# Queries, keys and normalised x turned by transposing DMAs in a layer with differential attention

## The reference

```python
x = x + 0.5 * ffn(layernorm(x))
x = x + attn(layernorm(x))
x = x + 0.5 * ffn(layernorm(x))
```

```python
q = rope((x @ Wq).reshape(b, s, H, 2 * D)); k = rope((x @ Wk).reshape(b, s, KVH, 2 * D)); v = x @ Wv
energy = einsum('bqhad,bkhad->bahqk', q.reshape(b, s, H, 2, D), k.reshape(b, s, H, 2, D))
scores = softmax(where(causal, NEG, energy) / sqrt(D))
diff = softmax(where(causal, NEG, scores[:, 0] - lam * scores[:, 1]))
att = einsum('bhqv,bvhd->bqhd', diff, v); att = att * rsqrt(mean(att * att) + EPS) * rms_w * (1 - LAM_INIT)
return att.reshape(b, s, E) @ Wo
```

## Time and profile before

| | us |
|---|---|
| median of 3 runs | 1826.18 (1823.63 to 1830.19) |
| the profiled execution, its own time | 1838.54 |
| its span | 1836.7 |
| TensorE busy | 1473.0 (80%) |
| VectorE busy | 1456.8 (79%) |
| ScalarE busy | 1260.1 (69%) |
| GpSimd busy | 1082.6 (59%) |
| mean granted TensorE clock, share of full | 0.863 |

### The profile page before, as it was taken

One profiled execution on the slowest core, in us unless ns is written; L12 is line 12 of the kernel. 1 busy time (PEld: TensorE's weight loads), 2 busy tenths in 40 slices (PEclk: granted clock), 3 DMA queues, 4 the chain that ended last, 5 costly groups with the idle time before them and its releaser, 6 DMA issues. The chain is left out here.

```text
span 1836.7 us, 43825 instructions
## 1 busy us (share of the span) xinstructions
PE 1473.0 (80%) x10688; PEld 1035.1 (56%) x10688; DVE 1456.8 (79%) x5505; ACT 1260.1 (69%) x3426; POOL 1082.6 (59%) x1493
## 2 busy tenths in 40 slices
PE   3997645888898998889888898888988888888620
PEld 3543322666666666666666666666666666666310
DVE  5778425888889898898889988898989877674477
ACT  2363334888788888888888888888888876675320
POOL 4421443666677677776777777777777665554300
PEclk9998776788899899999999899998999887676855
DMA  8023321111111111121111111121211100001186
GB/s 304 2 64 135 118 66 42 29 32 36 32 46 46 44 50 50 44 50 44 44 44 44 44 44 50 46 52 45 51 46 45 42 19 21 19 17 41 41 312 252
DMA packets 179673, 117.30 MB, mean 64 GB/s; under 512 B 139169, under 2 KB 139553, under 8 KB 179618
## 3 DMA queue, kind: packets, MB, share of 16 engines
q1 hardware_dynamic: 179618, 116.65, 21.5%
HBM read 51.57 MB, written 33.55 MB: 46 GB/s over the span
## 5 line engine op out<-in xcount | busy, mean ns | idle before, releaser
L1675 ACT ACTIVATE ex<-bank,nbias 128x512 f32<-128x512 f32 (+3 forms) x1024 | 527.7, 538 | 83.2 <-DVE bank L1220 80.6
L1220 DVE TENSOR_SCALAR_CACHE_REDUCE bank<-bank,nesc 128x512 f32<-128x512 f32 (+3 forms) x1024 | 503.3, 551 | 84.6 <-PE bank L1930 83.9
L1960 PEld LDWEIGHTS bank<-vs,pr 128*128 128x128 f32 x2560 | 336.3, 207 | 24.5 <-issue 12.7
L1960 PE MATMUL bank<-vs,pr 128*128 (+1 forms) x2560 | 341.4, 284 | 9.8 <-DVE att L1266 5.3
L1942 PE MATMUL bank<-cst,df 128*128 128x128 f32 x1280 | 265.9, 310 | 83.6 <-ACT pr L1692 83.0
L1928 PE MATMUL bank<-ks,qs 96*128 (+2 forms) x1024 | 266.2, 337 | 68.7 <-ACT ex L1675 45.4
L1522 POOL TENSOR_SCALAR ex<-ex,gam 128x128 f32<-128x128 f32 (+3 forms) x512 | 317.3, 630 | 0.0
L1692 ACT ACTIVATE pr<-bank 128x128 f32<-128x128 f32 (+3 forms) x512 | 231.7, 453 | 88.5 <-PE bank L1942 87.3
L1246 DVE CUSTOM_DVE_ANT_0 df<-ex 128x128 f32<-128x128 f32 (+3 forms) x512 | 261.1, 525 | 8.2 <-issue 3.7
L1942 PEld LDWEIGHTS bank<-cst,df 128*128 128x128 f32 x1280 | 169.8, 167 | 111.0 <-ACT pr L1692 96.2
L1675 ACT ACTIVATION_READ_ACCUMULATOR ex<-bank,nbias 128x1 f32 x1024 | 222.6, 217 | 0.0
(11 more groups left out here) (359 smaller groups left out, 2954.5 us busy)
## 6 DMA issues: line engine op xcount, KB each, us to landing
qs<-turned SPq DMA_DIRECT2D x360, 64.0 KB, 2.1
x_dram<-xa SPq DMA_DIRECT2D x8, 1024.0 KB, 4.9
c_x<-x_dram SPq DMA_DIRECT2D x8, 1024.0 KB, 14.7
c_y<-y_dram SPq DMA_DIRECT2D x8, 1024.0 KB, 14.7
out_dram<-c_x SPq DMA_DIRECT2D x8, 1024.0 KB, 4.7
b_xs<-x_dram SPq DMA_DIRECT2D x30, 256.0 KB, 2.7
xa<-in_x SPq DMA_DIRECT2D x7, 1024.0 KB, 13.6
x<-x_dram SPq DMA_DIRECT2D x28, 256.0 KB, 2.6
```

Source lines behind the costliest of these rows:

```text
L1220: dve.tensor_scalar(part, part, nesc[:, 0:1], None, ALU.mult, ALU.min, accum_out=nbias[:, j, i, a:a + 1]).then_inc(bias_done.sem, 1)
L1675: ac.activation(ex[j % 4][:, a, lo:hi], energy(j, i)[:, a, :], ACT.Exp, bias=nbias[:, j, i, a:a + 1], scale=-1.0, accum_out=esum[:, j, i, ...
L1960: mm = pe.matmul(bank[:, 7, t * DV:(t + 1) * DV], pr[j % 2][:, lo + k * P:lo + (k + 1) * P], val, start=(k == 0), stop=(k == t))
```

## The change

The halves of x, of the queries and of the keys are turned by DMAs with the transposing flag. For queries and keys ScalarE and GpSimd write the halves in the order of the stack, four places of 32 numbers for each head and part (the fourth is filled with zeros once, ahead of everything), and one DMA turns 16 or 8 blocks of 128 x 128 straight into `qs` or `ks`. The transposes on TensorE, the copies out of PSUM, the buffer `turned` and the 24 stacking DMAs go. `stack_early` sends the first query piece in the middle of a body; the other two go at its end, and `turn_x` ahead of them. The halves of x lie in the buffer of the rotated queries (`rows`), the head norm and the second normalisation write in place, and the halves of heads and second x have a buffer of their own (`hsplit`).

```diff
-            split = sb2("split", [P, 2, NQ + NK], F16)
+            NB = (16, 16, 8)
+            split = [sb2(f"split{n}", [P, nb * P], F16) for n, nb in enumerate(NB)]
-            turned = sb2("turned", [P, 2, NC, P], F16)
+            rows = rot[:, :].bitcast(F16).rearrange("p (a n) -> p a n", a=2)
+            hsplit = sb2("hsplit", [P, 2, E], F16)
...
-            an = sb2("an", [P, E])
-            xn2, xt2 = an, at
+            xn2, xt2 = x2, at
+            def an(u):
+                return att[:, ds(u & 7, 1), :, 0:D].rearrange("p a h d -> p (a h) d")
...
+            def stacked(piece, n):
+                return piece.rearrange("p (b j d) -> p b j d", j=4, d=D)
+            def high_of(piece, n):
+                three_ = stacked(piece, n)
+                return three_[:, :, 0:3:2, :] if n < 2 else three_[:, :, 0:2, :]
+            def low_of(piece, n):
+                return stacked(piece, n)[:, :, 1 if n < 2 else 2, :]
+            def twice(ap, n):
+                return by_block(ap, n).unsqueeze(2).broadcast_to([P, NB[n], 2, D])
...
             @blk.sync
                 def load_again(u):
                     sp.wait_ge(x2_st, u * 16 + 16)
-                    xn2_done.wait(sp, u - 1, apart_s)
+                    lo2_done.wait(sp, u - 1, apart_s)
...
-                def stack(u, K, source=turned):
-                    ring, t = (u >> 2) & 1, u & 3
-                    if K is not None:
-                        e_done.wait(sp, 2 * pair(K, STEPS - 1) + 1)
-                    turned_out.wait(sp, u * 3 + 2, apart_s)
-                    for dst, order, c0, c1, done in ((qs, (0, 1, 0), 0, CQ, stacked_q),
-                                                     (ks, (0, 0, 1), CQ, NC, stacked_k)):
-                        to = dst[:, :, :].rearrange("p (r c i) (t s) -> p r c i t s", r=2, i=4, s=P)
-                        for j, part in enumerate(order):
-                            for i in range(4):
-                                sp.dma_start(to[j * D:(j + 1) * D, ds(ring, 1), :, i, ds(t, 1), :]
-                                             .rearrange("p r c t s -> p (r c) (t s)"),
-                                             source[i * D:(i + 1) * D, part, c0:c1, :]).then_inc(done, 16)
+                def turn_rows(out, source, done):
+                    for a in range(2):
+                        sp.dma_start(out[:, a, :].rearrange("p (k n) -> p k n", k=KT),
+                                     source[:, a, :].rearrange("p (k n) -> p k n", k=KT), transpose=True).then_inc(done, 16)
+                def turn_x(u):
+                    proj_done.wait(sp, 3 * u - 1, apart_s)
+                    lo_done.wait(sp, u, apart_s)
+                    turn_rows(xt, rows, xt_in)
+                def turn_part(n, ring, t, source, done):
+                    dst, first = ((qs, 0), (qs, 16), (ks, 0))[n]
+                    to = dst[:, :, :].rearrange("p (r b) (t s) -> p r b t s", r=2, s=P)[:, ds(ring, 1), first:first + NB[n],
+                                                                                       ds(t, 1), :]
+                    sp.dma_start(to.rearrange("p r b t s -> p (r b) (t s)"), source.rearrange("p (b n) -> p b n", n=P),
+                                 transpose=True).then_inc(done, 16)
+                def stack_early(u, K):
+                    e_done.wait(sp, 2 * pair(K, -1) + 1, apart_s)
+                    rlo_done.wait(sp, 3 * u, apart_s)
+                    turn_part(0, (u >> 2) & 1, u & 3, split[0][:, :], stacked_q)
+                def stack(u, K):
+                    e_done.wait(sp, 2 * pair(K, STEPS - 1) + 1, apart_s)
+                    rlo_done.wait(sp, 3 * u + 2, apart_s)
+                    turn_part(1, (u >> 2) & 1, u & 3, split[1][:, :], stacked_q)
+                    turn_part(2, (u >> 2) & 1, u & 3, split[2][:, :], stacked_k)
...
+                def turn_first(u):
+                    if u >= 2:
+                        proj_done.wait(sp, 3 * (u - 2) + 2, apart_s)
+                    lo_done.wait(sp, u, apart_s)
+                    turn_rows(p_xt[u % 2], p_rows[u % 2], first_xt[u % 2])
                 def stack_first(u):
-                    for done in (stacked_q, stacked_k):
-                        sp.wait_ge(done, u * 192 + 16)
-                    stack(u, None, p_turned[u % 2])
+                    for n in range(3):
+                        rlo_done.wait(sp, 3 * u + n, apart_s)
+                        turn_part(n, u // TB, u % TB, p_split[u % 2][n], first_stack[u % 2])
...
+                sp.wait_ge(pads_set, 6)
                 load_first(0)
                 load_first(1)
                 load_again(0)
+                turn_first(0)
+                load_first(2)
+                turn_first(1)
+                load_first(3)
...
-                load_first(2)
-                load_first(3)
+                turn_first(2)
+                load_first(4)
                 stack_first(0)
-                load_first(4)
+                turn_first(3)
                 stack_first(1)
+                turn_first(4)
...
                 def finish(K, load_next, again, u):
                     if load_next:
                         load(K + (AHEAD + 1))
+                    if u is not None:
+                        stack_early(u, K)
                     store(K - BEHIND)
                     if again:
                         load_again(K - (BEHIND - 1))
                     store_y(K - BEHIND)
+                    if load_next:
+                        turn_x(K + (AHEAD + 1))
                     if u is not None:
                         stack(u, K)
...
             @blk.vector
+                for two in p_split:
+                    for n in range(3):
+                        dve.memset(two[n].rearrange("p (b n) -> p b n", n=P)[:, :, K3:P], 0.0).then_inc(pads_set, 1)
...
                 def head_norm(u):
                     ri_done.wait(dve, u)
-                    lo2_done.wait(dve, u - 1)
...
                 def normalise2(u):
                     rstd2_done.wait(dve, u)
                     al_done.wait(dve, u)
+                    dve.wait_ge(x2_st, u * 16 + 32)
...
             @blk.gpsimd
                     def f(u):
                         rhi_done.wait(gp, 3 * u + n)
-                        cols = slice(n * 512, n * 512 + width)
-                        gp.tensor_tensor(split[:, 1, cols], rot[:, 0:width], split[:, 0, cols], ALU.subtract)\
-                          .then_inc(rlo_done.sem, 1)
+                        gp.tensor_tensor(low_of(split[n][:, :], n), by_block(rot[:, 0:width], n), stacked(split[n][:, :], n)[:, :, 0, :],
+                                         ALU.subtract).then_inc(rlo_done.sem, 1)
...
             @blk.scalar
                 def high(tau):
                     xn_done.wait(ac, tau)
-                    rt_done.wait(ac, 3 * tau - 2)
-                    ac.copy(split[:, 0, ROWS], xn[:, :]).then_inc(hi_done.sem, 1)
+                    ac.wait_ge(xt_in, tau * 32)
+                    rlo_done.wait(ac, 3 * tau - 1)
+                    ac.copy(rows[:, 0, :], xn[:, :]).then_inc(hi_done.sem, 1)
...
                         rope_done.wait(ac, 3 * tau + n)
-                        rt_done.wait(ac, 3 * (tau - 1) + n)
...
-                        ac.copy(split[:, 0, n * 512:n * 512 + width], rot[:, 0:width]).then_inc(rhi_done.sem, 1)
+                        ac.wait_ge(stacked_q if n < 2 else stacked_k, tau * (32 if n < 2 else 16) + 16)
+                        ac.copy(high_of(split[n][:, :], n), twice(rot[:, 0:width], n)).then_inc(rhi_done.sem, 1)
...
             @blk.tensor
                     def f(u):
-                        xt_out.wait(pe, u)
-                        if n > 0:
-                            rope_v.wait(pe, 3 * u + n - 1)
-                        if n == 2:
-                            turned_out.wait(pe, 3 * u)
+                        pe.wait_ge(xt_in, u * 32 + 32)
+                        rope_v.wait(pe, 3 * u + n - 1)
+                        if n == 0:
+                            v_done.wait(pe, u - 1)
```

More of the change, by code:

```diff
@@ L1059, in program @@
             last_in = [sem2(f"last_in{q}") for q in range(CLOSE)]
-            first_in = [sem2(f"first_in{u}") for u in range(AHEAD)]
+            first_in, first_xt, first_stack = ([sem2(f"{n}{i}") for i in range(2)]
+                                               for n in ("first_in", "first_xt", "first_stack"))
             x1_t = x1_d.rearrange("b (t p) e -> (b t) p e", p=P)
@@ L1160, in _ @@
                 stack_first(3)
+                for u in range(TB):
+                    stacked_first(u)
                 stack_first(4)
+                stacked_first(4)
+                turn_x(AHEAD)
                 with sp.Fori(0, BEHIND) as K:
                     load(K + (AHEAD + 1))
+                    stack_early(K + AHEAD, K)
+                    turn_x(K + (AHEAD + 1))
                     stack(K + AHEAD, K)
@@ L1726, in high_heads @@
```

(22 more changed lines are left out.)

180 lines of the change are left out of this document (46 added, 134 removed).

## The result

The changed kernel takes 1852.74 us (median of 4 runs, 1845.04 to 1860.59) against 1825.88 for the kernel before beside it: ratio **1.0133, with an interval from 1.0094 to 1.0171**. It is slower by 1.3%, where 1777 us was forecast. In a few sets some executions fell into a slower state of the chip: the medians here count all executions, the ratios leave those out, and so a ratio is not always the quotient of two medians.

What follows compares the result with a forecast made beforehand. VectorE was taken to bound the loop, DMA issuing the stretch before the first energies. 22 us in the prologue plus 27 in the loop took the median from 1826 to 1777 us; forecast's own range 1738 to 1805, 8-in-10 range 1738 to 1960.

Steps and rivals of the forecast that it cites:

- a granted clock: Loop: clock averaging 0.94, left out of the sum; could move 27 bodies up to 30 us either way; moving meant wrong.
- the loop's 27 us: Loop: less TensorE and ScalarE work frees 1.0 us of VectorE's waits a body, over 27 bodies; ends 0 and 62 us.
- 2.3 us a body: Loop: VectorE's waits for TensorE's energies and weighted values, 31.8 us in 14 bodies, taken as the ceiling of any gain.
- The prologue, 22 us won: Before the loop: first energies at 266 us in place of 288.4, as turned blocks replace the stacking DMAs.
- The six fills: Prologue: SyncE waits for six fills of padding before loading anything, so the load goes 2 to 5 us later; 4 taken.
- my own line for T = 0.15: Prologue: at 0.15 us for each turned block, computing is the limit, first energies about 262 us, 26 us won.
- T = 0.28 us a block: Transposing DMAs: time to turn one 128 x 128 block, from the mean packet price of 35 ns; bounds 0.15 and 0.61 us.
- The block-by-block rival: SyncE's queue: each block issued like its own DMA at 0.61 us, total 1950 us; chance 0.20.
- the one with a round trip for each block: DMAs: turned blocks don't overlap, each paying its own way; at 1.8 us a block near 3300 us; chance 0.11.
- The four waits for DMAs: Next tile's x, next queries' cast, second normalisation and prologue wait for DMAs; the three in the loop in time at 0.28 us.
- the first of the four: Loop, x of the next tile: turned by 1019.8 us, 1.0 us before the first projection needs it.
- The new wait of ScalarE: Loop: ScalarE's cast of x waits 1.1 us for GpSimd's last low half; ScalarE's 2.7 us saving pays for it.

Runs made afterwards that it cites:

- e2: Kernel before with 4 of its 28 loop transposes a body left, ScalarE copying a constant in place of the turned blocks; 1847.52 us, ratio 1.0065.
- e13: Changed kernel with 56 useless TensorE transposes a body, GpSimd's last low half left in its slot; 1794.18 us, ratio 0.9792.
- e15: Changed kernel as it is, measured again in a later set; 1849.8 us, ratio 1.0095 to the kernel before.
- e14: Kernel before with the change made in the prologue alone and the old loop kept, second measurement; 1805.96 us, ratio 0.9856.
- e3: Changed kernel with GpSimd's last low half of the keys made one slot earlier; 1844.27 us, ratio 1.0052.
- e4: Changed kernel with 28 useless transposes a body and GpSimd's last low half one slot earlier; 1818.92 us, ratio 0.9915.
- e1: Changed kernel with 28 useless transposes a body at the places of the old ones; 1830.64 us, ratio 0.998.
- e8: Changed kernel with 56 useless transposes a body and GpSimd's last low half one slot earlier; 1789.95 us, ratio 0.9785.
- e12: Changed kernel with 56 useless transposes a body and the earlier low half, measured again; 1807.54 us, ratio 0.9824.

## Why the prediction was wrong

**The step that failed** is in the last lines of the prediction: a granted clock "which the sum leaves alone", and which could move 27 bodies by up to 30 us up or down. It was treated as noise from outside. The runs show that taking transposes from TensorE moves it: over the 21 bodies from 0.94 to 0.92 with the change, and to 0.89 when 24 transposes a body go from the kernel before (e2, 0.65% slower). With 56 put into the changed kernel it is 0.99 there, and they are worth 3.0% (e13 against e15, 55 us), nearly twice the bound I had set. The prediction had named a clock that moves as a sign of being wrong, and that sign came.

**The term that went with it** is the loop's 27 us. I had read VectorE's waits for TensorE, 2.3 us a body, as time that less work on TensorE and ScalarE would free. For the most part they were the clock's. In the body of the earlier trace rows at full clock, the kernel before waits for TensorE only this much:

```profile
DVE bank L1220 <- PE bank L1930: 0.4, 1, 0.4
```

So where the clock was full there was next to nothing to win, and where it was not the change made it worse.

The Trainium skill ("TensorE: Matmul & The Clock Gate", Part 4: PE-mode transpose) says that the full clock doesn't engage for transposes, which don't count as busy time in the same way. These runs disagree: with nothing but transposes added, the granted clock of the 600 us went from 0.92 to 1.00.

Step by step:
- *The prologue, 22 us won.* Right in kind, undersized: 28.6 us in the profile, 1.44% alone (e14, 27 us). The six fills delayed the load by 1.6 us, not 4, and the first projection (201.38 us) came with the one of before (200.85). With the blocks cheaper than I took, computing was the limit: my own line for T = 0.15 had said about 262 us. (The forecast's upper end, 1805, was too low by my own line: it was to hold up to T = 0.35, where 200 blocks end at 280 us and the sum gives 1818.)
- *T = 0.28 us a block.* Too high. The views of the changed kernel for the stack's source line (ns of one issue) and its landing:

```profile
L1140 SPq DMA_TRANSPOSE qs<-split x60: 1487/1838/3449, 221.8 to 1459.6; - x60
```

```profile
qs<-split SPq DMA_TRANSPOSE x60, 4.3
...
b_xt<-rot SPq DMA_TRANSPOSE x54, 2.5
```

  16 blocks land in 4.3 us where T = 0.28 wanted 6.5; less the 2 us of a landing it is 2.3 / 16 = 0.14 us, at my lower bound. My reason for 0.28, that a turned piece can't be cheaper than the kernel's mean packet, was wrong. The block-by-block rival is out (16 blocks at 0.61 us would be 9.8 us), and so is the one with a round trip for each block. The Trainium skill's rate ("DMA: Bandwidth & Descriptors", Latency and other measured facts), which the prediction put at 0.13 us a block, agrees with this trace; its 1309 ns for one transpose by DMA ("VectorE: DVE Perf Modes", The three transpose paths) is no price per block here.
- *The four waits for DMAs.* Right from the second body on. x was turned from 1016.55 us with 2.51 us of issuing (I had put 0.7), and the projections still found it there. In the first body the first of the four came up, 6.60 us on TensorE and 10.13 on VectorE, since the turn of x stands there behind the stacks of five tiles. I had costed that place for a steady body only.
- *ScalarE.* -62.0 us where 73 were expected. The price of a tile was right: the doubled cast takes 1047 ns (taken: 1052), the short one 673, and the durations of the loop's casts and copies fall by 72 us. The busy time falls by less because in these traces one ScalarE instruction often starts before the last has ended, and it counts the overlap once:

```profile
L1774 ACT CAST split<-rot 128x1024 f16<-128x1024 f32 x54 | 56.6, 1047 | 16.7 <-POOL rot L1649 16.7
...
L1774 ACT CAST split<-rot 128x512 f16<-128x512 f32 x27 | 18.2, 673 | 0.0
```

- *The new wait of ScalarE* was foreseen at 1.1 us and is 1.54. "ScalarE has won 2.7 us to pay for that" holds in the steady bodies, with the earlier low half or without. In the first bodies it doesn't: there the wait costs some 10 us (e3, and e4 against e1: 0.65%, same chip, intervals apart), except with 56 transposes (e13).
- *The loop, 27 us won.* In place of that it lost 2.4% (44 us, e15 against e14). At full clock the 2.3 us a body that I had called the ceiling is gone from VectorE's waits (e13), but so it is in the kernel before. And the body at full clock takes 42.7 us, not 41, and is longer than the 41.82 of the earlier trace rows, with VectorE busy 40.5 us in place of 39.53 for the same number of instructions. Its group of tiny products by `lam`, before and in e13 (700 to 1300 us):

```profile
L1234 DVE SCALAR_TENSOR_TENSOR gam<-esum,lam,rsum 128x2 f32<-128x2 f32 x110 | 55.2, 502 | 15.3 <-DVE rsum L1227 11.4
```

```profile
L1294 DVE SCALAR_TENSOR_TENSOR gam<-esum,lam,rsum 128x2 f32<-128x2 f32 x113 | 69.1, 611 | 15.5 <-DVE rsum L1287 12.0
```

  That is 8 x 0.11 = 0.9 us a body. What holds them longer was not tried. e13 stays 0.6% under e14 (12 us, intervals that just touch), but that compares a clock of 0.99 with one of 0.93. That the change by itself is worth anything in the loop no run shows.

What stays open: e1 has all 28 transposes back and is still 1.2% above e14, where the loop is the old one. By the table 11.5 us of this lie ahead of the first copy, and e4 shows that these are the wait for GpSimd; 9.6 lie in the 21 bodies, where the clock is 0.92 against 0.93, and were not taken apart.

## What to carry to other kernels

Before taking work off TensorE, whose clock moved with its load here, read the granted clock of the stretch and ask what holds it up; a saving on TensorE is not a saving where the bound engine waits for TensorE's next product. If a lighter TensorE makes a kernel slower, put useless transposes into its idle slots as a test: it costs ten lines, and may be the fix, up to a dose that must be measured. Run two doses in the same slots, so that the waits are the same and only the work differs, and look at where in the kernel the time goes: here 28 gave time back in the first bodies, and only 56 did in the steady ones. The doses 0, 28, 56 and 112 gave 1.005, 0.992, 0.979 to 0.982 and 0.989 of the kernel before, with the earlier low half. A wait is worth the time only where nothing else is late: before counting VectorE's waits for TensorE as a gain, look at them in a stretch at full clock. And a change with two places should be run in each alone: here the prologue's half was a clean 1.4%, hidden under the loop's loss.

## What the runs showed of the hardware

- Transposing DMAs between SBUF tiles: an issue holds SyncE's queue 1.24 us for 4 blocks and 1.84 us for 16, and 16 blocks (512 KB) land in 4.3 us. In the changed kernel they raise the DMA engines' share of the steady loop only from 0.18 to 0.26.
- The half clock and the body lengths repeat together. The changed kernel, e3 and e4 all run steady bodies of 44.4 us, equal to 0.1 us, although their waits differ; the kernel before repeats five lengths (42.5, 45.0, 42.7, 44.2 and 44.0 us). In the changed kernel even the last bodies, which prepare no tile, take 44.4 (the copies of e15 run from 529.3 to 1727.3, as in the first profile within 2 us). In e8 and e13 these last bodies, with no useless transpose in them, take 40 to 42 us (all but the very last), and in e12, the same kernel as e8, 44.4 to 44.9 again. 27 bodies from first to last copy take 1159.1 us in e8's profile and 1178.7 in e12's, and 16.5 us of the difference lie in the last six. It is most of what lies between the two profiled executions of this one kernel (1789.34 and 1811.57 us). I read it so: the work that the half clock falls on delays the body, and the delay decides what it falls on in the next. No run tested that.
- Before the clock fell in the changed kernel, TensorE had been busy for 2.13 of 3.40 us; it then ran at 1.2 GHz for 6.7 us, in every body. With 16, 16, 16 and 8 transposes of 0.07 us each in four slots (16 in 1.06 us in e13's timeline) the granted clock between 700 and 1300 us was 1.00, the 2.4 GHz level, while with the same 56 and GpSimd's low half one slot earlier it was 0.96 (e8). With half as many in the same slots it was 0.92 (e1), as with none. The dose is not all there is to it.
